# One of two x planes of a sampling step read back replicated from memory, the other double buffered in PSUM

## The chip, the cores and the metric

The kernel runs on one NeuronCore of a Trainium2 chip. The metric is the device time of one execution in microseconds (us). TensorE is called PE in the profile (its weight loads PEld), VectorE DVE, ScalarE ACT, GpSimd POOL and SyncE SP. SP issues the DMAs here.

## The reference

Four layers are added one after another onto x, of shape (4, 64, 48, 48), each on the group-normalised x: a deformable convolution (layer 1), two deformable convolutions that are mixed (layer 2), an attention (layer 3) and a convolution with generated weights (layer 4). The change is in layer 2, whose sampling is, cut to what matters:

```python
# offsets: B, 9 taps, (dy, dx), H, W, from a 3x3 convolution of x; twice, with two sets of weights
py = base_y + tap_y + dy;  px = base_x + tap_x + dx
sampled = bilinear_gather(x, py, px)          # B, C, 9, H, W; zero outside the image
out = einsum('bckhw,ock->bohw', sampled, w) + b
# the two results s0 and s1 are then mixed: wts0 * s0 + wts1 * s1 + conv1x1(x) * g
```

A bilinear gather is a sum over nearby pixels with the weight max(0, 1 - |y distance|) times max(0, 1 - |x distance|). The kernel uses this form where all offsets are small: every 4 x 6 tile of output pixels reads a window of 10 x 12 = 120 input pixels, and the gather is a matmul of the 120 window pixels with 120 x (pixels) weights.

## The kernel before

`windows1` works through 24 chunks of 8 rows of 48 pixels, so 384 pixels each (`CH`). There are 18 samples per pixel (9 taps of 2 convolutions), handled two at a time in 9 steps (`STEPS`).

**Hats.** For each chunk, PE computes the distances to the window's rows and columns for all samples ("place", line 1533, one matmul of 384 columns for each of 4 slots). ACT takes their magnitude (`magnitude`, 1617) into `temp`; POOL clips them (1705) and splits them into a high and a low f16 half (1708, 1710), the "hats". For the first chunk DVE does this (1662 to 1666). Hats are held compactly, 10 or 12 partitions for each sample, several samples to a slot and a group of 32 partitions.

**Spread** (1559). For step t PE replicates the y hats and the x hats of samples 2t and 2t+1 from 10 and 12 rows to the 120 window rows: four planes, each as a high and a low part, so eight matmuls of 32 rows x 120 columns in four row groups, four side by side. The y planes land in `p_y[t % 2]` (two banks each), the x planes in `p_x`, which has two banks and is single buffered.

**Weights.** A DVE operation can't take both factors from PSUM here, so ACT copies the first x plane to SBUF (`keep_x`, 1624), DVE copies the second (1672), and DVE then multiplies both y planes by both x planes in one operation of 768 columns (1677) into `bmat`.

**Sample** (1575). Eight times a chunk PE multiplies a pair of windows (loaded by SP at 1521 from `pixel_major` in DRAM) by the weights of the previous turn of `bmat`, into one of two banks `pq`, which the places use too; ACT moves the result to `smp` (`keep`, 1632).

**Conv** (1591) contracts 64 channels x 9 taps, 72 matmuls, into `pc` (in the banks of `p_y[1]`); ACT (1640) and DVE (1685) add the bias.

**Order.** All orders are written out by hand. PE runs, for chunk n: spread(n+1, t), sample(n, t), and after t in `PLACED = (0, 2, 4, 8)` a place for chunk n+2; then conv(n). ACT follows the same order with keep_x, keep and magnitude; DVE does the nine products of n+1 and then the bias of n; POOL has its own loop over the chunks and at the end normalises x again into `xn` for the next stage (1715). The spread waits for both copies of the step before:

```python
if g:
    pe.wait_ge(S["x0_out"], g)
    pe.wait_ge(S["x1_out"], g)
```

and conv(n) waits for the last keep, and for the products of n+1 up to the eighth. Of the places' turns and the samples' turns, each waits until the turn two before it has been emptied.

Of the kernel before, what the change touches and what calls it, by code (L numbers as in the profile page):

```python
# [4 lines left out]
F32 = mybir.dt.float32  # L5
U32 = mybir.dt.uint32
ALU = mybir.AluOpType
# [1439 lines left out]
def sample_slots():  # L1447


    groups = [(0, 1), (0, 2), (1, 2), (0, 3), (0, 1), (0, 2), (1, 3), (1, 2), (2, 3)]  # L1450
    places, rows = {}, {g: [] for g in range(4)}
    for axis, per, size in ((0, 3, IH + 6), (1, 2, IW + 6)):
        held = {g: [] for g in range(4)}
        for t, ys in enumerate(groups):
            own = ys if axis == 0 else [g for g in range(4) if g not in ys]
            for e, g in enumerate(own):
                held[g].append(2 * t + e)
# [6 lines left out]
    assert all(len(r) <= 4 for r in rows.values())  # L1464
# [3 lines left out]
def windows1(nc, k, o3, bmat, win, sc, smp, temp, xs):  # L1468
# [7 lines left out]
         ("loaded0", "loaded1", "hats0", "clipped0", "high0", "hats", "clipped", "high", "spread", "x0_out", "x1_out",  # L1476
          "weights", "filled", "emptied", "conv", "sc0", "sc1", "normed")}
# [4 lines left out]
    SLOTS = 4  # L1482
    places, _ = sample_slots()
    LAST = min(s // 2 for axis, s in places if places[axis, s][1] == SLOTS - 1)
# [9 lines left out]
    temp = temp.rearrange("p (q n) -> p q n", q=SLOTS)  # L1494

    PLACED = (0, 2, 4, STEPS - 1)

    def placing(n, t):

        return t in PLACED and n + 2 < NQ  # L1500

    turn_of = {("place", 0, q): q for q in range(SLOTS)}
    for n in range(-1, NQ):
        for t in range(STEPS):
            if n >= 0 and t < PAIRS:
                turn_of["sample", n, t] = len(turn_of)
            if placing(n, t):
                turn_of["place", n + 2, PLACED.index(t)] = len(turn_of)

    with nc.Block() as block:  # L1510
        @block.sync
        def _(sp):
            phased = k["xw"].rearrange("b y (j t) c -> b (y j) t c", j=IW)
            for n in range(NQ):
# [3 lines left out]
                for band in range(2):  # L1518
                    for a in range(2):
                        first = (ROWS * r + band * IH) * IW  # L1520
                        sp.dma_start(win[n % 2][KW // 2 * a:KW // 2 * (a + 1), band, :, :],
                                     phased[b, first:first + WH * IW, a:a + WW // IW, :]).then_inc(S[f"loaded{n % 2}"], 16)

        @block.tensor
        def _(pe):
# [10 lines left out]
            def spread(m, t):  # L1536
                g = m * STEPS + t
                held = SLOTS - 1 if t < LAST else SLOTS
                if m and t in (0, LAST):
                    pe.wait_ge(S["hats"], SLOTS * (m - 1) + held)  # L1540
                elif t in (0, LAST):
                    pe.wait_ge(S["hats0"], held)
                if g:
                    pe.wait_ge(S["x0_out"], g)
                    pe.wait_ge(S["x1_out"], g)
                if t < 2 and m:
                    pe.wait_ge(S["weights"], m * STEPS)
                elif t >= 2:
                    pe.wait_ge(S["weights"], g - 1)
                if t == 1 and m >= 2:  # L1550
                    pe.wait_ge(S["sc0"], m - 1)
                    pe.wait_ge(S["sc1"], m - 1)
                for part in range(2):
                    for axis in range(2):
                        for e in range(2):
                            row, slot, q = places[axis, 2 * t + e]
                            own = slice(32 * row, 32 * row + 32)
                            out = p_x[:, e, :] if axis else p_y[t % 2][:, e, :]
                            mm = pe.matmul(out, k["spr"][own, q, :], hat[m % 2][part][own, slot, :],  # L1559
# [1181 lines left out]
```

## Time and profile before

| what | value |
|---|---|
| runs (3), median | 1392.57 us |
| lowest, highest | 1387.49, 1393.74 us |
| profiled execution, span | 1386.4 us |
| PE busy | 1142.7 us |
| DVE busy | 983.5 us |
| ACT busy | 651.7 us |
| POOL busy | 696.3 us |
| first spread of the stage, end of its last instruction | 386.0 us, 788.5 us |

The profile gives the span of the profiled execution, from its first to its last recorded instruction, and no other time of it. The stage with the change takes 402 us of the 1386.4.

### The profile page before, as it was taken

Reading aid. Unit: us, or ns where it says so; the run is one execution under the profiler, and the core shown is the slowest. Engines: PE = TensorE matmul, PEld = TensorE weight load, DVE = VectorE, ACT = ScalarE, POOL = GpSimd, SP = SyncE. Lnnn points to the kernel's source line nnn. Section 1 sums busy time; section 2 is a strip of 40 time slices with the busy share of each in tenths; the row PEclk is TensorE's granted clock in tenths of the full one; section 3 lists DMA queues with packets and bytes.
Section 4 is the critical chain, followed back from the end, with each engine's and each line's share of the span. In section 5 each row is a group of like instructions: output and inputs, shape, how many; then the busy total and the mean of one; then the engine's idle time right before and its main releaser. Section 6 shows DMA issues by size and latency. Waiting matters only on the chain. (4 is left out here: it accounts for less than half of the span.)

```text
span 1386.4 us, 32503 instructions
## 1 busy us (share of the span) xinstructions
PE 1142.7 (82%) x13688; PEld 589.8 (43%) x13688; DVE 983.5 (71%) x1222; ACT 651.7 (47%) x1096; POOL 696.3 (50%) x549
## 2 busy tenths in 40 slices
PE   3970189869579999999999676699999999998658
PEld 2440177744225555555555443233333333334323
DVE  3788945567888888888888568746666666667623
ACT  1646035354546666666666535044444444445410
POOL 2000011203356767777676412078888888888600
PEclk9985599979769999999999889799999999999869
DMA  4100000001101111101111004000000000002002
GB/s 85 22 1 0 0 3 3 1 26 40 39 29 39 36 30 31 31 30 31 39 37 30 3 1 137 1 1 2 2 2 1 1 2 2 2 2 78 2 18 69
DMA packets 28884, 31.40 MB, mean 23 GB/s; under 512 B 19148, under 2 KB 21773, under 8 KB 27965
## 3 DMA queue, kind: packets, MB, share of 16 engines
q1 hardware_dynamic: 28573, 28.96, 7.9%
q8 instruction: 110, 1.80, 0.5%
q10 hardware_dynamic: 160, 0.30, 0.1%
q14 instruction: 41, 0.34, 0.1%
HBM read 20.91 MB, written 5.35 MB: 19 GB/s over the span
## 5 line engine op out<-in xcount | busy, mean ns | idle before, releaser
L2183 POOL TENSOR_TENSOR arena_sb<-arena_sb 128x768 f32<-128x768 f32 x168 | 322.5, 1920 | 119.6 <-ACT arena_sb L2144 99.1
L2144 ACT ACTIVATE arena_sb<-ps 128x768 f32<-128x768 f32 x216 | 175.0, 811 | 242.4 <-PE ps L2073 240.3
L2198 DVE TENSOR_REDUCE arena_sb<-ps 128x4 f32<-128x1536 f32 x108 | 188.2, 1756 | 128.8 <-PE ps L2040 128.3
L1677 DVE TENSOR_TENSOR arena_sb<-ps,arena_sb 120x768 f32<-120x768 f32 x216 | 206.8, 957 | 9.2
L2073 PE MATMUL ps<-arena_sb 33*64 33x384 f32 x1728 | 187.3, 502 | 11.4 <-ACT arena_sb L2144 5.5
L1705 POOL TENSOR_SCALAR xp_sb<-xp_sb 128x384 f32<-128x384 f32 x92 | 137.4, 1494 | 99.3 <-ACT xp_sb L1617 95.7
L1575 PE MATMUL ps<-arena_sb 120*64 120x216 f32 x1536 | 182.9, 360 | 0.0
L2085 PE MATMUL ps<-arena_sb 64*64 64x384 f32 x1728 | 168.0, 488 | 3.4 <-ACT arena_sb L2151 3.4
L1632 ACT ACTIVATE xp_sb<-ps 128x432 f32<-128x432 f32 x192 | 102.0, 531 | 63.1 <-PE ps L1575 63.1
L1559 PE MATMUL ps<-xn_sb,arena_sb 32*120 32x384 f16 x1728 | 120.8, 353 | 11.8 <-DVE arena_sb L1672 4.9
L1575 PEld LDWEIGHTS ps<-arena_sb 120*64 120x64 f32 x1536 | 93.4, 136 | 69.6 <-issue 32.9
L1672 DVE COPY arena_sb<-ps 120x384 f32<-120x384 f32 x216 | 118.8, 550 | 4.5 <-PE ps L1559 3.2
L2040 PE MATMUL ps<-arena_sb 32*128 32x384 f32 x864 | 104.6, 557 | 20.7 <-DVE arena_sb L2198 14.7
L1624 ACT ACTIVATE arena_sb<-ps 120x384 f32<-120x384 f32 x216 | 106.5, 493 | 17.6 <-PE ps L1559 14.0
L2073 PEld LDWEIGHTS ps<-arena_sb 33*64 33x64 f32 x1728 | 57.8, 134 | 110.4 <-ACT arena_sb L2144 86.2
L2085 PEld LDWEIGHTS ps<-arena_sb 64*64 64x64 f32 x1728 | 67.4, 134 | 78.8 <-issue 73.0
L1710 POOL TENSOR_TENSOR xn_sb<-xp_sb,xn_sb 128x384 f16<-128x384 f32 x92 | 84.5, 918 | 7.9
L1591 PE MATMUL ps<-xp_sb,arena_sb 64*64 64x192 f32 x1728 | 75.7, 325 | 6.1 <-DVE arena_sb L1677 5.5
L1559 PEld LDWEIGHTS ps<-xn_sb,arena_sb 32*120 32x120 f16 x1728 | 45.6, 129 | 76.3 <-ACT arena_sb L1624 45.9
L2040 PEld LDWEIGHTS ps<-arena_sb 32*128 32x128 f32 x864 | 35.6, 191 | 88.4 <-issue 44.9
L1591 PEld LDWEIGHTS ps<-xp_sb,arena_sb 64*64 64x64 f32 x1728 | 67.9, 133 | 11.7 <-ACT xp_sb L1632 11.5
L184 PE MATMUL ps<-x_sb,pairm_sb 128*128 128x256 f32 x56 | 22.2, 573 | 60.6 <-DVE arena_sb L573 60.6
(245 smaller groups left out, 1562.2 us busy)
## 6 DMA issues: line engine op xcount, KB each, us to landing
arena_sb<-pixel_major SPq DMA_DIRECT2D x96, 120.0 KB, 2.3
pixel_major<-arena_sb SPq DMA_DIRECT2D x24, 108.0 KB
x_sb<-in_x SPq DMA_DIRECT2D x4, 576.0 KB, 8.2
arena_sb<-arena_sb SPq DMA_DIRECT2D x8, 288.0 KB, 5.8
xn_sb<-in_W SPq DMA_DIRECT2D x1, 2304.0 KB, 8.0
arena_sb<-in_W SPq DMA_DIRECT2D x1, 2304.0 KB, 8.1
out_x<-x_sb SPq DMA_DIRECT2D x24, 96.0 KB, 2.2
arena_sb<-arena_sb SPq DMA_DIRECT2D x24, 1.5 KB
```

The source lines that it names most:

```text
L1559: mm = pe.matmul(out, k["spr"][own, q, :], hat[m % 2][part][own, slot, :], start=(part == 0), stop=(part == 1))
L1575: mm = pe.matmul(out[64 * v:64 * v + 64, :, :, IW * t:IW * t + IW], win[n % 2][0:KW, band, tile, :], weights[:, TAPS * v:TAPS * v + TAPS, ...
L1591: mm = pe.matmul(pc[v][64 * h:64 * h + 64, :], k["dws"][own, t, :], smp[own, at:at + CH // 2], start=(t == 0), stop=(t == TAPS - 1), skip_ ...
L1672: v_.tensor_copy(xs[t % 2][:, CH:2 * CH], p_x[:, 1, :]).then_inc(S["x1_out"], 1)
L1677: v_.tensor_tensor(bmat[m % 2][:, 2 * CH * t:2 * CH * t + 2 * CH].rearrange("p (e n) -> p e n", e=2), p_y[t % 2], xs[t % 2].rearrange("p ( ...
L1705: pool.tensor_scalar(temp[:, q, :], temp[:, q, :], UNIT, UNIT, ALU.min, ALU.subtract)\
L2040: mm = pe.matmul(p_m(m)[:, u, :], q4[own, CH * ib + PT * a:CH * ib + PT * a + PT], k4[own, CH * jc:CH * jc + CH], start=True, stop=True)
L2073: mm = pe.matmul(p_scores(g)[64 * i:64 * i + 64, h, :], kp[own, key:key + 64], qp[own, PIX * b2 + CH * ib:PIX * b2 + CH * ib + CH], start= ...
L2085: mm = pe.matmul(p_o[64 * h:64 * h + 64, i, :], at[64 * i:64 * i + 64, b2 * TPI + j, 64 * h:64 * h + 64], pt[g % SLOTS][64 * i:64 * i + 64 ...
L2144: act.activation(pt[g % SLOTS].rearrange("p (h n) -> p h n", h=2), p_scores(g), ACT.Exp)\
L2183: pool.tensor_tensor(acc, first, pt[g % SLOTS], ALU.add).then_inc(S["pool_added"], 1)
L2198: v.tensor_reduce(part.rearrange("p (a u j) -> p a u j", a=3, u=NB)[:, a, :, jc], p_m(m), AX.X, ALU.max)\
```

## The change

One of the two x planes of a step takes another way to the 120 window rows.

- The x hats of the nine odd samples ("far") get one slot of their own, 12 x 9 = 108 partitions of 384 values in f32. SP stores them in DRAM (`far_hats`) and reads them back in three blocks of three steps, each block in two DMAs of 60 partitions, with the source repeated ten times (`to_broadcast`), so that they arrive in SBUF on all 120 window rows (`xd[0..2]`). One block is reused when the chunk before is through with it.
- The compact hats then need three slots instead of four. There are still four places a chunk: far at the end of step 0, slots 0 and 1 at the end of steps 2 and 4, slot 2 inside step 6, ahead of its sample.
- A spread has six matmuls instead of eight. Its one x plane lands in `p_x[g % 2]`, two banks used in turn, so it no longer waits for copies of the step before.
- DVE drops its copy and its 768-wide product, and makes two products of 384: the odd sample's with `xd`, the even one's with ACT's copy, which has four buffers instead of two.
- The conv's output moves to the two banks `pq`, and the wait for the bias of the last conv moves from spread(1) to sample(0).
- POOL's normalisation into `xn` at the end waits for the last product as well, since `xd[0]` and `xd[1]` lie in `xn`.

```diff
@@ windows1
-    p_x = ps[0:KW, 2048:3072].rearrange("p (e n) -> p e n", e=2)[:, :, 0:CH]
+    p_x = [ps[0:KW, 512 * (4 + i):512 * (4 + i) + CH] for i in range(2)]
-    pc = [ps[:, 512 * (2 + v):512 * (2 + v) + CH // 2] for v in range(2)]
+    pc = [ps[:, 512 * (6 + v):512 * (6 + v) + CH // 2] for v in range(2)]
-    PLACED = (0, 2, 4, STEPS - 1)
+    def tail(n, i):
+        return n + 2 < NQ and i in HEADS[0:SLOTS]
+    def head(n, i):
+        return n + 2 < NQ and i == HEADS[SLOTS]
+    HEADS = (0, 2, 4, 6)
+    ORDER = (SLOTS,) + tuple(range(SLOTS))
@@ sync
+            def far_away(m):
+                if m:
+                    sp.wait_ge(S["far"], m)
+                else:
+                    sp.wait_ge(S["far0"], 1)
+                if m >= 2:
+                    for blk in range(3):
+                        sp.wait_ge(S[f"far_in{blk}"], 32 * (m - 1))
+                sp.dma_start(far_dram[m % 2], far).then_inc(S["far_out"], 16)
+
+            def far_back(m, blk):
+                if blk == 0:
+                    sp.wait_ge(S["far_out"], 16 * (m + 1))
+                if m:
+                    sp.wait_ge(S["weights"], (m - 1) * STEPS + BLOCK * (blk + 1))
+                lines = far_dram[m % 2].rearrange("(e t) n -> e (t n)", e=WX)
+                for a in range(2):
+                    src = lines[IW * a:IW * a + IW, BLOCK * CH * blk:BLOCK * CH * blk + BLOCK * CH]
+                    sp.dma_start(xd[blk][KW // 2 * a:KW // 2 * (a + 1), :],
+                                 src.unsqueeze(0).to_broadcast([WH, IW, BLOCK * CH])).then_inc(S[f"far_in{blk}"], 16)
+
+            window(0)
+            window(1)
+            far_away(0)
+            for blk in range(3):
+                far_back(0, blk)
+            for n in range(-1, NQ):
+                if n >= 1 and n + 1 < NQ:
+                    window(n + 1)
+                if n + 2 < NQ:
+                    far_away(n + 2)
+                    for blk in range(3):
+                        far_back(n + 2, blk)
@@ tensor, spread
-                if g:
-                    pe.wait_ge(S["x0_out"], g)
-                    pe.wait_ge(S["x1_out"], g)
-                if t < 2 and m:
-                    pe.wait_ge(S["weights"], m * STEPS)
-                elif t >= 2:
+                if g >= 2:
                     pe.wait_ge(S["weights"], g - 1)
-                if t == 1 and m >= 2:
-                    pe.wait_ge(S["sc0"], m - 1)
-                    pe.wait_ge(S["sc1"], m - 1)
                 for part in range(2):
-                    for axis in range(2):
-                        for e in range(2):
+                    for axis, e in ((0, 0), (0, 1), (1, 0)):
...
@@ tensor, sample and conv
                 if i == 0:
                     pe.wait_ge(S["weights"], (n + 1) * STEPS)
                     pe.wait_ge(S[f"loaded{n % 2}"], 64 * (n // 2 + 1))
+                    if n:
+                        pe.wait_ge(S["sc0"], n)
+                        pe.wait_ge(S["sc1"], n)
...
                 pe.wait_ge(S["emptied"], turn_of["sample", n, PAIRS - 1] + 1)
-                if n:
-                    pe.wait_ge(S["sc0"], n)
-                    pe.wait_ge(S["sc1"], n)
-                pe.wait_ge(S["weights"], (n + 1) * STEPS + (STEPS - 1 if n + 1 < NQ else 0))
@@ scalar
+                if q == SLOTS:
+                    if m:
+                        act.wait_ge(S["far_out"], 16 * m)
+                    act.activation(far, pq[u % 2][0:FAR, 0:CH], ACT.Abs).then_inc(S["emptied"], 1)
+                    return
...
-                if g >= 2:
-                    act.wait_ge(S["weights"], g - 1)
-                act.activation(xs[t % 2][:, 0:CH], p_x[:, 0, :], ACT.Copy).then_inc(S["x0_out"], 1)
+                if g >= XS:
+                    act.wait_ge(S["weights"], g - XS + 1)
+                act.activation(xs[g % XS], p_x[g % 2], ACT.Copy).then_inc(S["x0_out"], 1)
@@ vector, weight
-                v_.wait_ge(S["spread"], g + 1)
-                v_.tensor_copy(xs[t % 2][:, CH:2 * CH], p_x[:, 1, :]).then_inc(S["x1_out"], 1)
-                v_.wait_ge(S["x1_out"], g + 1)
-                v_.wait_ge(S["x0_out"], g + 1)
...
+                if at == 0:
+                    v_.wait_ge(S[f"far_in{blk}"], 32 * (m + 1))
+                v_.wait_ge(S["spread"], g + 1)
+                own = bmat[m % 2][:, 2 * CH * t:2 * CH * t + 2 * CH]
+                v_.tensor_tensor(own[:, CH:2 * CH], p_y[g % 2][:, 1, :], xd[blk][0:KW, CH * at:CH * at + CH], ALU.mult)
+                v_.wait_ge(S["x0_out"], g + 1)
+                v_.tensor_tensor(own[:, 0:CH], p_y[g % 2][:, 0, :], xs[g % XS], ALU.mult).then_inc(S["weights"], 1)
@@ gpsimd
+                pool.wait_ge(S["emptied"], turn_of["place", m, SLOTS] + 1)
+                pool.tensor_scalar(far, far, 1.0, 1.0, ALU.min, ALU.subtract).then_inc(S["far"], 1)
...
             pool.wait_ge(S["spread"], NQ * STEPS)
+            pool.wait_ge(S["weights"], NQ * STEPS)
```

`sample_slots` deals the samples anew over the groups of 32 rows, so that the three planes of a step always lie in three different groups.

## Rows read from the trace of the kernel before

**Rows 1.** The page: busy time of each engine over the span.

```profile
span 1386.4 us, 32503 instructions
PE 1142.7 (82%) x13688; PEld 589.8 (43%) x13688; DVE 983.5 (71%) x1222; ACT 651.7 (47%) x1096; POOL 696.3 (50%) x549
```

**Rows 2.** Busy time by window, two chunks from conv to conv.

```profile
core 0: us, PE busy (x) PEld busy (x) DVE busy (x) ACT busy (x) POOL busy (x), PEclk, DMA share, GB/s
546.54:562.70 16.16, 15.84 (x212) 8.93 (x212) 13.82 (x21) 10.63 (x25) 11.66 (x12) 1.00 0.11 32
562.70:578.87 16.17, 15.84 (x212) 8.94 (x213) 13.83 (x21) 10.63 (x25) 11.66 (x12) 1.00 0.11 32
```

**Rows 3.** Timeline, a chunk's end (start us, us, what, idle before it); one spread's first half.

```profile
556.32 0.95 PE L1575 MATMUL ps<-arena_sb 120*64 120x216 f32 x8
...
557.21 0.34 PE L1533 MATMUL ps<-arena_sb 109*128 109x384 bf16 x1
...
557.47 0.54 PE L1559 MATMUL ps<-xn_sb,arena_sb 32*120 32x384 f16 x8
...
557.94 0.95 PE L1575 MATMUL ps<-arena_sb 120*64 120x216 f32 x8
...
558.83 0.54 PE L1559 MATMUL ps<-xn_sb,arena_sb 32*120 32x384 f16 x8
...
559.59 0.55 DVE L1672 COPY arena_sb<-ps 120x384 f32<-120x384 f32 x1
...
560.21 0.22 PEld L1559 LDWEIGHTS ps<-xn_sb,arena_sb 32*120 32x120 f16 x8 [0.35 <-ACT arena_sb L1624]
...
560.71 0.95 PE L1575 MATMUL ps<-arena_sb 120*64 120x216 f32 x8
...
561.05 0.55 DVE L1672 COPY arena_sb<-ps 120x384 f32<-120x384 f32 x1
...
561.66 0.22 PEld L1559 LDWEIGHTS ps<-xn_sb,arena_sb 32*120 32x120 f16 x8 [0.39 <-ACT arena_sb L1624]
...
561.71 0.53 ACT L1632 ACTIVATE xp_sb<-ps 128x432 f32<-128x432 f32 x1 [0.39 <-PE ps L1575]
...
562.17 0.34 PE L1533 MATMUL ps<-arena_sb 109*128 109x384 bf16 x1
...
562.73 3.16 PE L1591 MATMUL ps<-xp_sb,arena_sb 64*64 64x192 f32 x72 [0.23 <-DVE arena_sb L1677]
...
565.82 0.54 PE L1559 MATMUL ps<-xn_sb,arena_sb 32*120 32x384 f16 x8
...
565.95 0.85 ACT L1640 ACTIVATE arena_sb<-ps,dbs_sb 64x192 f32<-64x192 f32 x2 [2.79 <-PE ps L1591]
...
566.29 0.95 PE L1575 MATMUL ps<-arena_sb 120*64 120x216 f32 x8
...
541.31 0.38 PE L1559 MATMUL ps<-xn_sb,arena_sb 32*120 32x384 f16 x4
```

**Rows 4.** Groups by line: an operation of DVE as wide as the new products.

```profile
L1342 DVE TENSOR_TENSOR arena_sb<-ps,arena_sb 108x384 f32<-108x384 f32 x24 | 11.7, 550 | 5.6 <-PE ps L1269 5.2
```

**Rows 5.** Timeline, the end of the stage.

```profile
772.27 16.28 POOL L1715 TENSOR_SCALAR xn_sb<-x_sb,stats_sb 128x2304 f32<-128x2304 f32 x2 [12.04 <-PE ps L1559]
...
776.73 0.53 ACT L1632 ACTIVATE xp_sb<-ps 128x432 f32<-128x432 f32 x1
777.31 0.56 PEld L1575 LDWEIGHTS ps<-arena_sb 120*64 120x64 f32 x8 [0.29 <-ACT xp_sb L1632]
...
786.01 0.85 DVE L1685 TENSOR_SCALAR arena_sb<-ps,dbs_sb 64x192 f32<-64x192 f32 x2 [9.30 <-PE ps L1591]
```

**Rows 6.** DMAs: issues, windows while window loads run, packets of the first eight.

```profile
381.30 3.50 SPq L1521 DMA_DIRECT2D arena_sb<-pixel_major  x8
...
arena_sb<-pixel_major SPq DMA_DIRECT2D x96, 120.0 KB, 2.3
arena_sb<-arena_sb SPq DMA_DIRECT2D x8, 288.0 KB, 5.8
...
547.00:549.00 2.00, 2.00 (x56) 2.00 (x52) 0.88 (x1) 0.00 (x0) 1.85 (x2) 1.00 0.62 193
381.00:385.00 4.00, 1.70 (x4) 0.34 (x4) 2.73 (x7) 1.74 (x4) 0.00 (x0) 0.50 0.57 170
...
DMA packets 600, 0.98 MB, mean 164 GB/s; under 512 B 120, under 2 KB 120, under 8 KB 600
```

**Rows 7.** Timeline, the stage's first and ninth product and its first sample.

```profile
387.72 0.96 DVE L1677 TENSOR_TENSOR arena_sb<-ps,arena_sb 120x768 f32<-120x768 f32 x1
...
400.77 0.96 DVE L1677 TENSOR_TENSOR arena_sb<-ps,arena_sb 120x768 f32<-120x768 f32 x1
...
401.85 0.31 PEld L1559 LDWEIGHTS ps<-xn_sb,arena_sb 32*120 32x120 f16 x8 [1.68 <-issue]
402.71 1.01 PEld L1575 LDWEIGHTS ps<-arena_sb 120*64 120x64 f32 x8 [0.55 <-issue]
```

More of the change, by code:

```diff
@@ L1447, in sample_slots @@
 def sample_slots():
-    groups = [(0, 1), (0, 2), (1, 2), (0, 3), (0, 1), (0, 2), (1, 3), (1, 2), (2, 3)]
+    steps = [(0, 1, 2), (0, 1, 3), (0, 2, 1), (1, 2, 0), (0, 3, 1), (1, 3, 0), (0, 1, 2), (0, 3, 2), (1, 2, 3)]
     places, rows = {}, {g: [] for g in range(4)}
-    for axis, per, size in ((0, 3, IH + 6), (1, 2, IW + 6)):
+    for axis, per in ((0, 3), (1, 2)):
         held = {g: [] for g in range(4)}
[L1454 to L1457, printed above, removed]
+        for t, (first, second, across) in enumerate(steps):
+            for g, s in ((first, 2 * t), (second, 2 * t + 1)) if axis == 0 else ((across, 2 * t),):
+                held[g].append(s)
         for g in range(4):
@@ L1463, in sample_slots, with windows1 @@
                     places[axis, s] = (g, slot, q + 3 * axis)
-    assert all(len(r) <= 4 for r in rows.values())
+    assert all(len(r) <= SPREAD_SLOTS for r in rows.values())
     return places, rows
-def windows1(nc, k, o3, bmat, win, sc, smp, temp, xs):
+SPREAD_SLOTS = 3
+FAR = WX * TAPS
+def windows1(nc, k, o3, bmat, win, sc, smp, temp, xs, xd):
     ps = k["psum"]
     S = {n: signal(k, "win_" + n) for n in
-         ("loaded0", "loaded1", "hats0", "clipped0", "high0", "hats", "clipped", "high", "spread", "x0_out", "x1_out",
-          "weights", "filled", "emptied", "conv", "sc0", "sc1", "normed")}
+         ("loaded0", "loaded1", "hats0", "clipped0", "high0", "far0", "hats", "clipped", "high", "far", "far_out",
+          "far_in0", "far_in1", "far_in2", "spread", "x0_out", "weights", "filled", "emptied", "conv", "sc0", "sc1",
+          "normed")}
     NQ = NB * CPI
@@ L1513, in _, with window @@
             phased = k["xw"].rearrange("b y (j t) c -> b (y j) t c", j=IW)
-            for n in range(NQ):
+            def window(n):
                 b, r = divmod(n, CPI)
@@ L1659, in _ @@
         def _(v_):
+            v_.wait_ge(S["emptied"], turn_of["place", 0, SLOTS] + 1)
+            v_.tensor_scalar(far, far, 1.0, 1.0, ALU.min, ALU.subtract).then_inc(S["far0"], 1)
             for q in range(SLOTS):
@@ L2709 @@
                     selp[R3, slot, at] = -e
+    for e in range(WX):
+        for t in range(TAPS):
+            selp[0:R3, SPREAD_SLOTS, TAPS * e + t] = row == 2 * (2 * t + 1) + 1
+            selp[R3, SPREAD_SLOTS, TAPS * e + t] = -e
     for q in range(3):
```

100 lines of the change are left out of this document (58 added, 42 removed).

## The prediction

> **What bounds the kernel now.** The page first [rows 1]: TensorE (PE) is busy 82% of a 1386.4 us span, VectorE (DVE) 71%. The change touches only layer 2's sampling, so I went from the page to the busy time by window over two of its 24 chunks [rows 2]: one chunk takes 16.16 us, and in it PE is busy 15.84, DVE 13.82, ACT 10.63, POOL 11.66, at full granted clock. PE's 0.3 us of idle is not all of its slack, since the pace of matmuls that wait for weights doesn't show as idle. So the third view is the timeline of the end of one chunk [rows 3], read for the distance from the start of one PE group to the start of the next:
>
> - sample to place 0.89 (556.32 to 557.21), place to spread 0.26, spread to sample 0.47, sample to spread 0.89 (557.94 to 558.83) where nothing holds it.
> - In the two steps without a place the last distance is 0.95 and 0.99. There the weight load of the spread starts at 560.21 and 561.66, right behind the end of the copy of the second x plane (559.59 + 0.55 = 560.14; 561.05 + 0.55 = 561.60). This is the single x buffer: the spread may not overwrite `p_x` before both copies are out. DVE meanwhile runs copy and product end on end, one step per 1.46 us.
> - At the chunk's end place to conv takes 0.56 instead of 0.26, until DVE's product at line 1677 lets go.
> - The conv to the next spread takes 3.09, and sample(0) follows 0.47 later, before the two bias operations (565.95 to 566.80) are done.
>
> The unheld sum of a chunk is conv 3.09 + 9 spreads x 0.47 + 8 samples x 0.88 + 4 places x 0.265 = 15.42 (the finer end of 0.88 to 0.89 and 0.26 to 0.27 is taken; with 0.89 it is 15.5). Against 16.16 the waits on DVE's copies and products are worth 0.7 us a chunk, 17 us over 24 chunks. That is all the change can win in the steady part by relieving DVE.
>
> **Steps that are taken off DVE and PE.** DVE loses the copy (0.55) and its 768-wide product (0.96) and gets two products of 384 columns; the nearest row with one PSUM and one SBUF operand and 384 columns is 0.55 [rows 4], so 1.10 or less instead of 1.51, 3.7 us a chunk. That is no gain by itself: PE is then alone on the path. A spread goes from eight matmuls to six, but they are four (now three) side by side in two rounds: the first four of one spread take 0.38 us together and a single place with the same 384 columns 0.34 [rows 3], so a matmul more or less in a round costs (0.38 - 0.34)/3 = 0.013. Its bounds: 0, and 2 x 0.013 x 216 = 5.7 us won over the kernel. I take 0, since the distance from spread to sample (0.47) is the same as from spread to place and looks set by two rounds and a drain, not by the count.
>
> The Trainium skill ("TensorE: Matmul & The Clock Gate", Part 3, Measured speedup vs the span model) says that row tiles side by side cost one matmul plus about 4 ns for each further tile. By that rule the removed pair is worth 8 ns a spread, an estimate of 1.7 us in all, and the trace's 0.38 against 0.34 is of that order.
>
> **Waits that are added.** The conv's output moves from `p_y`'s banks to the two banks `pq` in which samples and places land. Two things follow.
>
> - sample(0) of the next chunk now waits for both biases of the conv. They start 3.22 after the conv (565.95 against 562.73) and last 0.85, so they end at +4.07; a weight load starts 0.05 after such a release (776.73 + 0.53 = 777.26, load at 777.31 [rows 5]). sample(0) starts at +4.12 instead of +3.56: 0.56 us of PE with nothing behind it to fill, because spread(1) is queued behind sample(0).
> - The conv still waits for ACT's keep of sample(7), which ends 1.53 after that sample's start (560.71 to 561.71 + 0.53 = 562.24). Up to now a spread (0.89 + 0.47) and a place (0.26) filled 1.62. The place of step 8 moves to the head of step 6, so only 1.36 is filled, and with 0.06 to 0.08 of release the conv starts 1.60 after the sample: 0.24 lost.
>
> New chunk: 15.42 + 0.56 + 0.24 = 16.22, with the coarse sum 16.30; I take 16.26, 0.10 more than now. Over the 22 chunks that have both a conv behind and spreads ahead: +2.2 us. Bounds of this term: 16.16 - 0.2 if the rounds get cheaper, which is -4, and 16.16 + 0.3 (+7) if the coarser distances hold and ACT, which has a magnitude and a keep_x ahead of keep(6), holds sample(6) up by a tenth.
>
> **Work at no cost, and its cover.** POOL has three slots (1.49 + 0.50 + 0.92 each) and one 1.49 for the far planes, 10.2 us instead of 11.66; the last slot, placed at step 6, is done about 1.4 us before the next chunk begins, and is needed at its step 2 only. ACT has the same number of operations. SP gets one store and six reads more per chunk (about 0.5 us of issue each, by 8 issues in 3.50 us [rows 6]); window(n+1) stands behind them but has a whole chunk of cover. The read-back moves 6 x 276 KB a chunk. Its first pair can start once the far store has landed, about 10 us after the conv, and is needed at about 20 us; the later pairs have 11. A 120 KB load lands in 2.3 us, a 288 KB transfer of another layer in 5.8 [rows 6]: hidden either way. If the cover were gone, each microsecond beyond it would cost 22.
>
> **The ends of the stage.** Before the first product the far planes must go out and come back. SP issues eight window loads first (381.30 to about 385.2), then the store (landing 2.3, at 387.5), then the first pair. With 553 KB at the 193 GB/s of a window stretch (2.9 us), and 1.7 for a landing's fixed part (2.3 less 0.6 for its 120 KB) [rows 6], they land about 4.7 us later, at 392.2, where now the first product starts at 387.72 and the ninth ends at 401.73 [rows 7]. Nine steps at 1.05 end at 401.7, and spread(1,0) need no longer wait for all nine (now it starts at 401.85), so sample(0) goes from 402.71 to 401.7: -1 us. Bounds: -3.4 (the pair lands in 2.3) to +2.5 (the store takes 5.8). At the other end POOL's normalisation, 16.28 us from 772.27 to 788.55, ends the stage, 1.7 us after ACT and DVE (786.01 + 0.85) [rows 5]. It waits now for the last spread and will wait for the last product too: two products of 0.55 more, +1.1. The 0.6 us that the last chunk's sample(0) waits and the conv's 0.24 lie under it.
>
> Sum: +2.2 - 1.0 + 1.1 = +2.3 us on a span of 1386.4. The profile gives no other time of that execution; the median of the runs is 1392.57, 6.2 above the span, and I carry that over: 1394.9, say 1395.
>
> **The rivals.**
>
> - *The wait was worth more than its replacement* (faster). If spreads of three tiles are quicker by the share of instructions removed, 2/8 of 0.47 = 0.12 a spread, 216 of them save 25 us: 1370. At the upper bound from the rows above (5.7) it is 1389. For it: PE is what paces the new chunk. Against it: the 0.38 beside 0.34. Chance 0.18, most of it between 1375 and 1386.
> - *The read-back paces the chunk* (slower). 480 KB of windows, 166 KB out and 1656 KB back are 2.3 MB in 16.26 us, 141 GB/s. The stretches of window loads show 193 GB/s at a DMA share of 0.62, and 170 in one that starts idle [rows 6]. It decides below 141 GB/s; at 120 a chunk takes 19.2 us and the kernel 1395 + 22 x 2.9 = 1459. For it: reads whose source repeats ten times are in no row of this kernel. Against it: both stretches of window loads are above the limit though SP issues only one 120 KB load per half microsecond in them, and a read-back carries 276 KB per issue. Chance 0.10, with a few small stalls of DVE (each under 1 us a chunk, to 1415) in it.
> - *ACT comes late* (slower): in the steps with a place sample(i+1) starts 0.05 behind the release of keep(i), so anything ahead of a keep costs its full length. A tenth at four places a chunk is 0.4 x 23 = 9 us: 1404. Chance 0.12.
> - *The change trades nothing visible*: the forecast, 0.60, with its own range 1388 to 1400.
>
> The page that speaks against the change is "DMA: Bandwidth & Descriptors" of the Trainium skill (Rules for kernel authors): a leading zero-stride broadcast of c copies confines a DMA to at most c engines, here ten. The trace agrees as far as it goes: the eight window loads, 60 rows each, carry 120 packets under 512 B, 15 each, the largest divisor of 60 up to 16. By that rule the read-back runs at ten sixteenths of 193/0.62 = 311 GB/s, an estimate of 195 GB/s: 8.5 us a chunk for the 1656 KB, which would not change the sum; did it bind, the time would be the second rival's.
>
> **How the numbers follow.** The likeliest case gives 1395. The range 1383 to 1405 takes in the bounds of the terms (-4 to +7 for the chunks, -3 to +3 for the start, -5.7 for the rounds) and the ACT case, and leaves out most of the first and second rival. About 0.5%, 7 us, is what a measurement of this kernel can tell from no change: faster than 1385.6 has 0.18, slower than 1399.5 has 0.24 (0.10 + 0.12 + the forecast's own tail), the rest 0.58.
>
> **What would show it.** In the changed profile: conv to conv 16.2 to 16.3; copies gone and DVE about 10 us busy a chunk; the weight load of sample(0) held for 0.5 to 0.6 us by the biases of ACT and DVE, that of the conv by ACT's keep; spread to sample still 0.47; DMA share 0.3 to 0.5 with no DVE wait on a DMA after the first chunk; POOL's normalisation starting 1.7 us after the last spread. The prediction is wrong if spread to sample falls below 0.45, if DVE waits for a DMA in each chunk, or if sample(0) isn't held.

## The result and the profile after

The changed kernel takes 1401.56 us (median of 7 runs, 1397.21 to 1401.63), the kernel before 1391.75 in the same comparison (7 runs, 1387.14 to 1394.44). The ratio is 1.0067, 95% interval 1.0048 to 1.0086: slower by 0.67%, 6.7 to 12 us. The prediction was 1395 within 1383 to 1405. The time lies inside, 6.6 above the centre, and falls under "slower by over 0.5%", which had been given 0.24 against 0.58 for no visible change.

The page of the changed kernel answers to [rows 1]; the profiled execution took 1401.58, 1.8 above its span:

```profile
span 1399.8 us, 31420 instructions
PE 1143.0 (82%) x13256; PEld 589.2 (42%) x13256; DVE 901.1 (64%) x1220; ACT 646.2 (46%) x1096; POOL 664.5 (47%) x503
```

DVE lost 82 us of work and the profiled span is longer. Busy time by window over two chunks from conv to conv, against [rows 2]:

```profile
core 0: us, PE busy (x) PEld busy (x) DVE busy (x) ACT busy (x) POOL busy (x), PEclk, DMA share, GB/s
541.50:557.92 16.42, 15.55 (x195) 8.66 (x195) 10.56 (x21) 10.38 (x24) 10.23 (x11) 1.00 0.51 149
557.92:574.34 16.42, 15.55 (x194) 8.66 (x194) 10.56 (x21) 10.38 (x24) 10.23 (x11) 1.00 0.48 140
```

A chunk takes 16.42 us where 16.26 was predicted and 16.16 was the time before; DVE went from 13.82 to 10.56, 3.3 less, where 3.7 and "about 10" were said. PE is busy 0.29 less and idle 0.87 instead of 0.32. The timeline shows where, from one conv (L1635) over the first samples (L1623) to the next conv:

```profile
541.50 3.15 PE L1635 MATMUL ps<-xp_sb,arena_sb 64*64 64x192 f32 x72 [0.16 <-ACT xp_sb L1684]
...
544.58 0.54 PE L1604 MATMUL ps<-xn_sb,arena_sb 32*120 32x384 f16 x6
544.72 0.85 ACT L1692 ACTIVATE arena_sb<-ps,dbs_sb 64x192 f32<-64x192 f32 x2 [2.85 <-PE ps L1635]
544.72 0.85 DVE L1743 TENSOR_SCALAR arena_sb<-ps,dbs_sb 64x192 f32<-64x192 f32 x2 [2.26 <-PE ps L1635]
...
545.79 0.59 PEld L1623 LDWEIGHTS ps<-arena_sb 120*64 120x64 f32 x8 [1.03 <-issue]
545.82 0.95 PE L1623 MATMUL ps<-arena_sb 120*64 120x216 f32 x8 [0.71 <-DVE arena_sb L1743]
...
547.44 0.95 PE L1623 MATMUL ps<-arena_sb 120*64 120x216 f32 x8
...
548.79 0.95 PE L1623 MATMUL ps<-arena_sb 120*64 120x216 f32 x8
...
556.34 0.95 PE L1623 MATMUL ps<-arena_sb 120*64 120x216 f32 x8
...
557.22 0.54 PE L1604 MATMUL ps<-xn_sb,arena_sb 32*120 32x384 f16 x6
557.34 0.53 ACT L1684 ACTIVATE xp_sb<-ps 128x432 f32<-128x432 f32 x1 [0.39 <-PE ps L1623]
...
557.92 3.15 PE L1635 MATMUL ps<-xp_sb,arena_sb 64*64 64x192 f32 x72 [0.16 <-ACT xp_sb L1684]
```

Read it as three pieces. From conv to sample(0) 4.32 (541.50 to 545.82). From sample(0) to sample(7) 10.52, made of steps of 1.62 with a place and 1.35 without (545.82, 547.44, 548.79): that is 0.88 + 0.47, with 0.27 for a place, so nothing holds these steps any more. From sample(7) to the conv 1.58, released by ACT's keep (557.34 + 0.53 = 557.87). The first piece was priced at 4.12, and here the price is missed: the biases end at 545.57, 4.07 after the conv as forecast, but the weight load comes at 545.79, 0.22 behind them, not 0.05, and the first matmul 0.03 behind the load. (4.12 was the start of the load, while the 3.56 of before that it was set against is the start of the matmul; in the kernel before the two start together.)

The start of the stage in the timeline, against [rows 6] and [rows 7]:

```profile
385.42 0.81 PE L1587 MATMUL ps<-arena_sb 109*128 109x384 bf16 x2 [1.35 <-PEq L1372]
385.69 3.49 SPq L1541 DMA_DIRECT2D arena_sb<-pixel_major  x8
...
389.22 0.36 SPq L1552 DMA_DIRECT2D far_hats<-xp_sb  x1
...
391.99 3.28 SPq L1562 DMA_DIRECT2D xn_sb<-far_hats  x4
...
397.41 0.56 DVE L1735 TENSOR_TENSOR arena_sb<-ps,xn_sb 120x384 f32<-120x384 f32 x1 [6.69 <-DMA xn_sb<-far_hats]
...
406.78 0.28 PEld L1604 LDWEIGHTS ps<-xn_sb,arena_sb 32*120 32x120 f16 x6 [1.55 <-POOL xn_sb L1770]
...
407.61 1.01 PEld L1623 LDWEIGHTS ps<-arena_sb 120*64 120x64 f32 x8 [0.55 <-DVE arena_sb L1737]
...
409.00 0.56 DVE L1735 TENSOR_TENSOR arena_sb<-ps,xn_sb 120x384 f32<-120x384 f32 x1 [1.92 <-DMA xn_sb<-far_hats]
```

DVE waits 6.69 us for the first pair of read-backs. The code ahead of the stage is unchanged but its end scatters (the first place lay at 381.0 to 386.7 us in the profiles of this study), so all positions below count from the first place of the stage: sample(0) comes at 22.19, and came at 21.67 before. DVE's ninth product ends at 407.08, but sample(0) is queued behind spread(1,0), which waits until 406.78 for POOL's hats and takes 0.83 at the lower clock. So sample(0) starts at 407.61, 0.53 behind DVE's end; with 0.05 to 0.22 for a release, 0.3 to 0.5 of that is POOL's doing. Its end, against [rows 5]:

```profile
787.94 16.27 POOL L1776 TENSOR_SCALAR xn_sb<-x_sb,stats_sb 128x2304 f32<-128x2304 f32 x2 [14.19 <-DVE arena_sb L1737]
```

POOL's normalisation starts 1.63 us after the last spread (the start of its second round; 0.44 before), and from there to the end of the stage it takes 17.90 instead of 16.72.

### The profile page after: what moved, and what is told of

The parts are those of the page before. It is cut to its first block and busy times, and to the rows that moved or that the text cites. A ratio compares the mean times of both kernels' runs of the same rounds, so it can differ in the third digit from the quotient of the medians.

```text
span 1399.8 us, 31420 instructions
## 1 busy us (share of the span) xinstructions
PE 1143.0 (82%) x13256; PEld 589.2 (42%) x13256; DVE 901.1 (64%) x1220; ACT 646.2 (46%) x1096; POOL 664.5 (47%) x503
## 5 line engine op out<-in xcount | busy, mean ns | idle before, releaser
L1623 PE MATMUL ps<-arena_sb 120*64 120x216 f32 x1536 | 185.8, 364 | 16.8 <-DVE arena_sb L1743 16.8
L1623 PEld LDWEIGHTS ps<-arena_sb 120*64 120x64 f32 x1536 | 96.6, 138 | 85.4 <-issue 44.2
L1765 POOL TENSOR_SCALAR xp_sb<-xp_sb 128x384 f32<-128x384 f32 x69 | 103.0, 1493 | 48.9 <-ACT xp_sb L1669 45.1
L1735 DVE TENSOR_TENSOR arena_sb<-ps,xn_sb 120x384 f32<-120x384 f32 x144 | 80.3, 558 | 70.0 <-PE ps L1604 60.7
L1737 DVE TENSOR_TENSOR arena_sb<-ps,arena_sb 120x384 f32<-120x384 f32 x216 | 120.2, 556 | 1.1
L1758 POOL TENSOR_SCALAR xp_sb<-xp_sb 108x384 f32<-108x384 f32 x23 | 34.4, 1494 | 96.0 <-ACT xp_sb L1663 96.0
L1635 PE MATMUL ps<-xp_sb,arena_sb 64*64 64x192 f32 x1728 | 75.7, 325 | 4.4 <-ACT xp_sb L1684 4.4
L1604 PEld LDWEIGHTS ps<-xn_sb,arena_sb 32*120 32x120 f16 x1296 | 41.6, 131 | 71.0 <-issue 63.1
L1635 PEld LDWEIGHTS ps<-xp_sb,arena_sb 64*64 64x64 f32 x1728 | 63.7, 133 | 16.5 <-ACT xp_sb L1684 12.8
```

What stands on the lines that cost most here:

```text
L1623: mm = pe.matmul(out[64 * v:64 * v + 64, :, :, IW * t:IW * t + IW], win[n % 2][0:KW, band, tile, :], weights[:, TAPS * v:TAPS * v + TAPS, ...
L1635: mm = pe.matmul(pc[v][64 * h:64 * h + 64, :], k["dws"][own, t, :], smp[own, at:at + CH // 2], start=(t == 0), stop=(t == TAPS - 1), skip_ ...
L1737: v_.tensor_tensor(own[:, 0:CH], p_y[g % 2][:, 0, :], xs[g % XS], ALU.mult).then_inc(S["weights"], 1)
L1765: pool.tensor_scalar(temp[:, q, :], temp[:, q, :], UNIT, UNIT, ALU.min, ALU.subtract)\
```

## The experiments

Theory A: the two waits that the conv brought with it into `pq` eat the gain, and sample(0)'s release costs 0.17 more than it was priced at. Theory B: the read-back's traffic slows what lies beside it (0.50 of the DMA engines busy at 142 GB/s, where it was 0.11 and 32 [rows 2]). A third, A2, was for the first profile's chunk 0: TensorE came to its full granted clock 15.0 us after sample(0), against 4.4 before, and the theory is that its idle time while DVE waits for the read-back delayed the clock. e1 to e4 and e7 to e9 are edits to the changed kernel; e5 builds on e1, and e6 on e5. In all of them `p_x` and `p_y` stay twice buffered. Where an edit has one run, its effect is read from the distances in its trace and not from its time.

**e1_conv_home: the conv back in two banks of `p_y`.** With it the waits go back: spread(1) waits for the biases, spread(0) and the conv for the products that empty the banks.

```diff
-    pc = [ps[:, 512 * (6 + v):512 * (6 + v) + CH // 2] for v in range(2)]
+    pc = [ps[:, 512 * (2 + v):512 * (2 + v) + CH // 2] for v in range(2)]
...
+                if t < 2 and m:
+                    pe.wait_ge(S["weights"], m * STEPS)
+                if t == 1 and m >= 2:
+                    pe.wait_ge(S["sc0"], m - 1)
+                    pe.wait_ge(S["sc1"], m - 1)
...
-                        out = p_x[g % 2] if axis else p_y[g % 2][:, e, :]
+                        out = p_x[g % 2] if axis else p_y[t % 2][:, e, :]
...
-                    if n:
-                        pe.wait_ge(S["sc0"], n)
-                        pe.wait_ge(S["sc1"], n)
```

> The changed kernel with the conv's output put back into the banks of the second y buffer and the wait for the bias back in spread(1), so sample(0) no longer waits for it; the y buffers go by the step's number again. The rest of the change stays. Theory A (the two banks of the conv cost the chunk its gain): in the changed kernel's trace sample(0) starts 4.32 us after the conv, here 3.55, so a chunk takes 15.65 us instead of 16.42, 17 us less over 22 chunks: about 1385, 7 us below the kernel before. Theory B (the read-back, 1.66 MB a chunk, paces the stage): the wait moves to another place, a chunk stays at 16.4 and the time at 1401. If the conv's own wait for the products of step 7 bites, a chunk takes up to 15.9 and the kernel 1390.

Measured: 1384.4 us median (1379.19 to 1386.74) beside 1390.16 of before, ratio 0.9955 (0.9939 to 0.997). A chunk takes 15.65 us:

```profile
549.24 3.16 PE L1641 MATMUL ps<-xp_sb,arena_sb 64*64 64x192 f32 x72 [0.16 <-ACT xp_sb L1690]
...
552.33 0.54 PE L1609 MATMUL ps<-xn_sb,arena_sb 32*120 32x384 f16 x6
552.47 0.85 ACT L1698 ACTIVATE arena_sb<-ps,dbs_sb 64x192 f32<-64x192 f32 x2 [2.85 <-PE ps L1641]
...
552.79 0.38 PEld L1625 LDWEIGHTS ps<-arena_sb 120*64 120x64 f32 x6 [0.28 <-issue]
```

sample(0) starts at 552.79, while the biases of 552.47 still run: 3.55 after the conv, 0.77 earlier than the 4.32 of the changed kernel, and 0.77 is what the chunk became shorter by (16.42 to 15.65). The same read-backs and products now win. So the relief of DVE is worth what the prediction said (16.16 - 15.65 = 0.51 with 0.23 of the conv's wait still there), and the wait of sample(0) alone, 0.77, was larger than it.

**e2_bias_wait_last: the bias waits behind the wait for the sample's bank.**

```diff
-                    if n:
-                        pe.wait_ge(S["sc0"], n)
-                        pe.wait_ge(S["sc1"], n)
                 u = turn_of["sample", n, i]
                 empty(u)
+                if i == 0 and n:
+                    pe.wait_ge(S["sc0"], n)
+                    pe.wait_ge(S["sc1"], n)
```

> The changed kernel; only the order of sample(0)'s waits differs: the wait for the bias comes behind those for the weights, the window and the bank. In the changed kernel sample(0)'s weight load starts 0.22 us after the bias has ended, with two wait instructions 0.11 apart between them. If each wait instruction behind the late one costs, the load comes 0.11 to 0.17 earlier and a chunk takes 16.26 to 16.31 instead of 16.42: 2 to 4 us in all. If the 0.22 is a fixed price of this release, conv to conv stays at 16.42.

One run of 1398.54; a chunk takes 16.42 as before the edit:

```profile
555.52 0.85 ACT L1692 ACTIVATE arena_sb<-ps,dbs_sb 64x192 f32<-64x192 f32 x2 [2.85 <-PE ps L1635]
555.52 0.85 DVE L1743 TENSOR_SCALAR arena_sb<-ps,dbs_sb 64x192 f32<-64x192 f32 x2 [2.26 <-PE ps L1635]
...
556.59 0.23 PEld L1623 LDWEIGHTS ps<-arena_sb 120*64 120x64 f32 x4 [1.02 <-issue]
```

The biases end at 556.37, the weight load comes at 556.59, 0.22 later. The wait instructions of TensorE's queue in the trace tell why: the five waits of sample(0) stand as two in each of two wait instructions and one in the load itself. In the changed kernel both biases are in the first wait instruction; with this edit one of them is still there, and only the other is in the second. So the edit didn't do what it was meant to, and it says nothing on the price of a wait instruction; e9 does.

**e3_thin_read_back: only 128 of 1152 columns read back** for all chunks but the first (x planes incomplete, so the weights are other numbers).

```diff
+                    W_ = 128 if m else BLOCK * CH
...
-                                 src.unsqueeze(0).to_broadcast([WH, IW, BLOCK * CH]))
+                                 src.unsqueeze(0).to_broadcast([WH, IW, W_]))
```

> The changed kernel with the same DMAs and waits, but from the second chunk on each read-back brings 128 of the 1152 columns of its block (512 B instead of 4608 B a row), so most x weights of the odd samples are stale. Theory B: a chunk falls from 16.42 towards 15.5 us, 15 us or more in all. Theory A: the transfers are hidden, conv to conv stays at 16.42 within 0.02, and only the DVE wait of 1.9 us in the second chunk goes.

One run of 1400.99. Busy time by window over the steady part, the changed kernel first, then this one:

```profile
405.00:770.00 365.00, 345.72 (x4193) 189.85 (x4192) 231.23 (x439) 227.64 (x504) 226.22 (x223) 0.98 0.50 142
```

```profile
405.00:770.00 365.00, 345.59 (x4264) 191.11 (x4262) 234.89 (x446) 229.54 (x509) 230.68 (x227) 0.99 0.17 52
```

DMA falls from 0.50 to 0.17 of the engines and from 142 to 52 GB/s; conv to conv stays at 16.43, and of the DVE waits on a DMA only the 1.92 us one in chunk 0 goes. Theory B falls: these bytes are free here (the number of DMAs was left as it is).

**e4_clock_kept: twenty matmuls more in DVE's wait for the first read-back**, into a bank that a place overwrites.

```diff
+                    if n == -1 and i == 1:
+                        pe.wait_ge(S["emptied"], SLOTS + 1)
+                        for _ in range(20):
+                            pe.matmul(pq[1][:, 0:CH], k["selp"][:, 0, :], o3[:, 0:CH], start=True, stop=True)
```

> The changed kernel with 20 matmuls of 384 columns of no use put behind spread(0,1), in the 6.9 us in which TensorE waits for the first read-back. In the changed kernel the granted clock rises to full only 14.4 us after the first sample, in the kernel before 4.3 us after it, and from the first sample to the first conv it takes 18.8 us instead of 14.4. Theory A2 (the idle stretch for the read-back keeps the clock down): full clock by the first sample, first sample to first conv about 13 to 14.5 us, 4 to 6 us less in all. Rival (the clock rises late because a spread holds fewer matmuls, or by chance of its phase): first sample to first conv stays near 18.8.

One run of 1400.87. Windows of the stage's start (the column behind POOL's is the granted clock):

```profile
394.00:398.00 4.00, 3.58 (x16) 1.69 (x14) 0.00 (x0) 0.11 (x1) 1.33 (x1) 0.76 0.51 141
398.00:402.00 4.00, 1.40 (x16) 0.56 (x19) 3.00 (x7) 1.25 (x3) 0.29 (x1) 1.00 0.67 218
402.00:406.00 4.00, 3.85 (x29) 1.27 (x32) 3.76 (x8) 2.36 (x6) 3.77 (x4) 0.59 0.29 98
406.00:410.00 4.00, 2.81 (x20) 1.21 (x20) 2.01 (x4) 1.47 (x3) 3.70 (x5) 0.50 0.61 185
410.00:414.00 4.00, 4.00 (x29) 1.64 (x27) 2.33 (x5) 2.10 (x5) 2.46 (x3) 0.63 0.65 181
```

The extra matmuls bring the full clock 9.6 us after the first place, but it is gone again at 402.7 (16.4 after the first place) and comes back at 26.7, 4.2 after sample(0). e3, without such matmuls, has it 3.7 after its sample(0). So the late clock of the first profile is no necessary effect of the change, and A2 doesn't explain it; the repetitions below settle that.

**e5_home_place_last: e1, and the place back behind step 8**, where the conv's wait was filled.

```diff
-        return n + 2 < NQ and i in HEADS[0:SLOTS]
+        return n + 2 < NQ and i in HEADS
...
-    HEADS = (0, 2, 4, 6)
+    HEADS = (0, 2, 4, STEPS - 1)
```

> The kernel of the first experiment (conv in the y buffer's banks) with the fourth place back behind step 8, ahead of the conv, instead of inside step 6. There the conv of the first experiment must wait for ACT's keep of sample(7), 1.6 us behind that sample's start, while a spread fills only 1.36. If that wait is real and the place fills it, a chunk takes 15.42 us, the unheld sum of the prediction, instead of 15.65, and the kernel 5 us less: 1379. If the conv is held by the products instead, it stays at 15.65 and 1384.

1377.03 us median (1376.21 to 1379.12) beside 1391.33, ratio 0.9902 (0.9885 to 0.9918). The chunk's end:

```profile
545.54 0.95 PE L1625 MATMUL ps<-arena_sb 120*64 120x216 f32 x8
...
546.42 0.54 PE L1609 MATMUL ps<-xn_sb,arena_sb 32*120 32x384 f16 x6
...
546.89 0.34 PE L1587 MATMUL ps<-arena_sb 109*128 109x384 bf16 x1
...
547.16 3.16 PE L1641 MATMUL ps<-xp_sb,arena_sb 64*64 64x192 f32 x72
```

Spread and place now fill the whole way from sample(7) to the conv, which shows no idle time ahead of it. Conv to conv is 15.42, the unheld sum that the prediction had put together from single distances.

**e6_all_mended: e5, with e7's and e8's edits.** 

> The kernel above with two more edits: the first far store and its read-backs are issued ahead of the first eight window loads, and the first half of POOL's normalisation no longer waits for the last product (its half of the array holds no read-back block). Expected against the kernel above: 2 to 3 us off the start (the store goes out at about 1.5 us behind the first place instead of 3.8) and 1.2 us off the end: 1375 to 1377, about 1.1% below the kernel before. If the start is set by the clock and not by the read-back, only the 1.2 us at the end show.

1374.57 us median (1373.91 to 1379.31), ratio 0.9885 (0.9868 to 0.9901): the fastest version. The chunk is e5's 15.42, the stage 394.37 us long against 396.86 in e5. In both profiles the full clock comes at nearly the same place (36.0 and 36.2 us from the first place), so they can be compared from the start on: conv(0) is 1.3 earlier in e6, and the end gives the other 1.2.

**e7_norm_split: the first half of POOL's normalisation no longer waits for the last product.** In the edit the wait for `weights` moves into the loop, ahead of the second half only.

```diff
-            pool.wait_ge(S["weights"], NQ * STEPS)
             st = k["stats"]
             for b in range(2):
+                if b:
+                    pool.wait_ge(S["weights"], NQ * STEPS)
```

> The changed kernel with only the second half of POOL's normalisation waiting for the last product. In the changed kernel it starts 1.65 us behind the start of the last spread's last round and ends 18.1 us behind the last spread's start; before it was 16.9. Expected: 16.9 again, 1.2 us off the stage. If the end of the stage is set by TensorE's last conv instead, nothing is won.

One run of 1394.91. From the last spread to the end of the stage it takes 16.72 again, and POOL's row names the spread as its releaser:

```profile
781.31 16.27 POOL L1777 TENSOR_SCALAR xn_sb<-x_sb,stats_sb 128x2304 f32<-128x2304 f32 x2 [13.02 <-PE ps L1604]
```

**e8_far_first: the first far store and its read-backs ahead of the window loads.**

```diff
-            window(0)
-            window(1)
             far_away(0)
             for blk in range(3):
                 far_back(0, blk)
+            window(0)
+            window(1)
```

> The changed kernel with the first far store and its read-backs issued ahead of the first eight window loads. In the changed kernel the store goes out 3.8 us behind the first place, DVE's first product starts 12.0 us behind it, and the first sample 22.2. Theory: the first product comes 2.3 us earlier, at 9.7, and the first sample at about 20. Rival: POOL's hats of the second chunk hold spread(1,0) (it waited 1.55 us for them in the changed kernel), then the first sample comes less than 1 us earlier.

One run of 1400.21. The timeline:

```profile
388.06 3.28 SPq L1562 DMA_DIRECT2D xn_sb<-far_hats  x4
391.38 1.52 SPq L1562 DMA_DIRECT2D arena_sb<-far_hats  x2
392.95 4.07 SPq L1541 DMA_DIRECT2D arena_sb<-pixel_major  x8
394.08 0.56 DVE L1735 TENSOR_TENSOR arena_sb<-ps,xn_sb 120x384 f32<-120x384 f32 x1 [4.35 <-DMA xn_sb<-far_hats]
397.06 0.36 SPq L1552 DMA_DIRECT2D far_hats<-xp_sb  x1
403.85 3.15 SPq L1562 DMA_DIRECT2D xn_sb<-far_hats  x4
...
409.23 0.56 DVE L1735 TENSOR_TENSOR arena_sb<-ps,xn_sb 120x384 f32<-120x384 f32 x1 [5.49 <-DMA xn_sb<-far_hats]
```

The first product comes 9.64 us after the first place (384.44) instead of 11.99, and sample(0) at 19.84, 2.4 earlier. But the next chunk's store now goes out behind the eight window loads, 12.6 after the first place instead of 11.5. Its read-back follows 6.8 later, as it did in the changed kernel (6.6; only the stage's first store took 2.8), so DVE waits 5.49 us in chunk 0 and starts that product at 24.8 instead of 23.6. Whether anything is won by conv(0) this profile can't tell against e11 and e12: it is at 38.8 with the full clock 33.2 after the first place, they at 36.4 with the clock at 26.7 and 26.9. Beside the first profile of the changed kernel, whose clock was late too (37.1), conv(0) is 2.2 earlier. e6 against e5, with equal clocks, puts the gain of this edit at 1.3 in that version.

**e9_early_waits: two of the five waits ahead of sample(0) moved up in TensorE's queue**, ahead of the spread before it, where both have long been met.

```diff
                 if i == 0:
-                    pe.wait_ge(S["weights"], (n + 1) * STEPS)
-                    pe.wait_ge(S[f"loaded{n % 2}"], 64 * (n // 2 + 1))
+                    if n == 0:
+                        pe.wait_ge(S["weights"], (n + 1) * STEPS)
+                        pe.wait_ge(S[f"loaded{n % 2}"], 64 * (n // 2 + 1))
...
+                    if n > 0 and i == 0:
+                        pe.wait_ge(S["weights"], (n + 1) * STEPS)
+                        pe.wait_ge(S[f"loaded{n % 2}"], 64 * (n // 2 + 1))
```

> The changed kernel with sample(0)'s waits for the weights and the window moved ahead of spread(0) of the same turn, where both are met already (except in the first chunk). Behind the conv sample(0) then has three waits instead of five. In the run with the bias wait last nothing changed, and its trace showed why: the waits are packed two to a wait instruction, one of the two bias semaphores still in the first of them, and a second wait instruction 0.11 us behind it. If the number of wait instructions behind the late semaphore is the price, the load starts 0.11 us earlier and conv to conv falls from 16.42 to 16.31, 2.4 us in all. If not, it stays at 16.42.

One run of 1392.16; a chunk takes 16.27. Around sample(0):

```profile
549.62 3.15 PE L1636 MATMUL ps<-xp_sb,arena_sb 64*64 64x192 f32 x72 [0.16 <-ACT xp_sb L1688]
...
552.85 0.85 DVE L1747 TENSOR_SCALAR arena_sb<-ps,dbs_sb 64x192 f32<-64x192 f32 x2 [2.26 <-PE ps L1636]
...
553.77 0.56 PEld L1624 LDWEIGHTS ps<-arena_sb 120*64 120x64 f32 x7 [0.87 <-ACT arena_sb L1696]
```

The biases end at 553.70 and the load follows at 553.77, 0.07 behind them instead of 0.22. The chunk is 0.155 shorter, and all of it is here. One wait instruction stands between the late biases and the load where there were two, and it was reached early: the trace shows it from 551.88 to 553.74, with one of the biases in it and the other in the load.

**e10_before_again, e11_after_again, e12_home_last_norm: repetitions**, the kernel before once and the changed kernel twice (e12 too is the changed kernel without an edit, whatever its label says).

> The kernel before, once more with a profile, for the scatter of what the change doesn't touch. In its first profile the first place came 381.0 us after the start and the clock rose 4.4 us behind the first sample, with the first conv 36.1 us behind the first place. If the late clock is a matter of the execution and not of the change, some of these looks differ from the first by several us; conv to conv stays at 16.16.

> The changed kernel once more. In its first profile the clock rose 15.0 us behind the first sample and the first conv came 41.0 us behind the first place; in the second, fourth and seventh experiment, whose start is the same up to there, 36.5 to 37.9. Expected if it is a matter of the execution: 36.5 to 38 here; if it belongs to this kernel: 41. Conv to conv stays at 16.42.

> A second repetition of the changed kernel, for the same purpose: a third look at where the clock rises behind the first sample (15.0 us in the first) and at the place of the first conv (41.0 us); the same two outcomes.

Single runs of 1393.97 (before), 1397.83 and 1396.41 (changed); another run of before beside them took 1389.51. One window of chunk 0, in the first profile of the changed kernel and then in e11:

```profile
411.00:415.00 4.00, 4.00 (x23) 1.55 (x19) 1.79 (x4) 1.41 (x4) 0.86 (x1) 0.50 0.50 161
```

```profile
411.00:415.00 4.00, 4.00 (x42) 1.75 (x38) 2.82 (x6) 2.90 (x8) 2.31 (x3) 1.00 0.15 46
```

Granted clock 0.50 (the lower level, 1.2 GHz) in the one, 1.00 in the other, in the same program. The stage, in us from its first place:

| profile | sample(0) | full clock after sample(0) | conv(0) | conv to conv | last spread | end |
|---|---|---|---|---|---|---|
| before | 21.67 | 4.4 | 36.09 | 16.16 | 390.79 | 407.51 |
| e10 (before again) | 21.66 | 4.7 | 36.19 | 16.16 | 390.83 | 407.55 |
| changed | 22.19 | 15.0 | 41.01 | 16.43 | 400.89 | 418.79 |
| e11 (changed again) | 22.35 | 4.5 | 36.49 | 16.43 | 396.36 | 414.26 |
| e12 (changed again) | 22.28 | 4.4 | 36.37 | 16.43 | 396.15 | 414.05 |
| e8 | 19.84 | 13.4 | 38.81 | 16.43 | 398.60 | 416.49 |
| e5 | 23.74 | 12.2 | 41.12 | 15.42 | 378.97 | 396.86 |
| e6 | 19.77 | 16.4 | 39.82 | 15.42 | 377.66 | 394.37 |

With equal clocks the change costs 414.15 - 407.53 = 6.6 us in its stage. No run rules out that the change makes a late clock more frequent: both profiles of the kernel before have it early, and four of the twelve others (the first one, e5, e6 and e8) have it 12 us or more after sample(0), e1 11.8.

## Why the prediction was right or wrong

**Right: the mechanism, and the size of the relief.** The relief of DVE removes the holds inside the steps (every step from sample(0) to sample(7) is unheld), and two new waits give it back. The unheld sum of 15.42 was measured as such in e5; the conv's wait for the keep, 1.60 predicted, is 1.58; sample(0) is held by the biases.

**Wrong: the size of sample(0)'s release.** The term was "+4.12", with 0.05 from the end of the biases to the weight load, read off a load that waits for one ACT operation [rows 5]. Measured: 4.32, with 0.22 and the 0.03 from the load to its matmul. Five waits stand ahead of sample(0), both late ones in the first of two wait instructions; with two of the five moved ahead the distance is 0.07 (e9). The chunk came to 16.425, the 16.22 of its fine sum and these 0.20, instead of the 16.26 that was taken: 0.26 over the 16.16 before instead of 0.10. Over the 22 chunks this term is 5.8 instead of 2.2; in the profiles 21 distances of 0.26 make 5.5, and the distance from conv(21) to conv(22), in which no place stands, gave 0.6 back.

**Wrong: the start, by 1.6.** The step was "-1.0", by a first product 11.2 us after the first place. It comes at 11.99: the store took 2.8 to its read-back (389.22 to 391.99; 2.3 taken), the pair 5.4 (391.99 to 397.41) where 4.7 was taken. Nine steps of 1.07 follow, where 1.05 was said. And spread(1,0), said to be free of the products, waits 1.55 for POOL's hats (L1770), a wait that the sum left out and that costs sample(0) 0.3 to 0.5. sample(0) is at 22.2 to 22.4 in the three profiles of the changed kernel, +0.6 and inside the bounds of -3.4 to +2.5. Half of it doesn't reach conv(0), which is +0.3 in e11 and e12.

**Right: the rest.** Six matmuls cost what eight cost: spread to sample is 0.47 in both kernels. The Trainium skill ("TensorE: Matmul & The Clock Gate", Part 3, Measured speedup vs the span model) has about 4 ns for each further tile, 8 ns for the removed pair; the medians here are 471 ns with four tiles a round and 468 with three, so the trace has even less. The read-back is hidden (e3), with no DVE wait on a DMA after the first chunks. Where nothing but read-backs moves, over 553 to 557, it goes at 173 GB/s and a DMA share of 0.59, below the 195 of the prediction's estimate and still enough. The stretch holds 20 packets under 512 B, 10 for each of two landings, where a window load has 15, which fits the prediction's ten engines. The tail is +1.2 (17.90 - 16.72), +1.1 predicted, and e7 takes it back. All four steps with a place take 1.62, the unheld 0.88 + 0.27 + 0.47, so the rival of ACT fell too, as did that of cheaper spreads.

**The account.** Predicted in the stage: +2.2 - 1.0 + 1.1 = +2.3. Measured with equal clocks: +0.3 to conv(0), +4.8 from there to conv(22), +1.5 behind that (the tail's 1.2 in it), 6.6. The medians are 9.8 apart. The remaining 3.2 is not settled. The first profile had 4.6 us more ahead of conv(0) with the late clock, and its time, 1401.58, is one of four at 1401.6 while the other three are at 1397.2 to 1399.4; that these four all had the late clock was not shown, and a time like theirs doesn't need it: e3 and e4, with the clock at 3.7 and 4.2 and stages of 414.1 us, took 1400.99 and 1400.87. In the profiles the code ahead of the stage differs by up to 5.7 us and what follows it by up to 5.1 (595.5 to 600.6), more than the 3.2 to be explained. Single runs of the kernel before also lie 4.5 apart (1389.51 and 1393.97). Of the 6.6 between centre and result, 4.3 are mis-sized terms; the rest is the unsettled 3.2, less the 0.8 by which the kernel before was faster in this comparison. The chances failed by how near the centre stood to the bound: with the 6.6 of the stage it would have been 1392.57 + 6.6 = 1399.2, at the edge of 1399.5. The time lies inside the range with or without the unsettled part. The range was 22 us wide for the sake of rivals that didn't come, so that it held says little of the sum.

## What to carry to other kernels

When an engine is relieved, look at where the freed buffer came from: here the second x bank cost the conv its own banks, and one hold of 0.77 us a chunk and 0.23 of the conv's wait that a moved place no longer filled cost more than the 0.74 us of relief. The same relief with the conv left in banks that are empty anyway gave 0.45%, 1.0% with the place left in the conv's wait, and 1.15% with start and end mended. Price a release not only by the end of the work waited for but also by the wait instructions between the late wait and the instruction, and move the waits that have long been met to an earlier instruction. A work item that fills a wait is worth its length only where it stands.

## What the runs showed of the hardware

- Waits of TensorE's queue have a price. From the end of the last bias to the weight load: 0.05 us with one wait [rows 5], 0.07 in e9 with three waits, 0.22 with five, in the changed kernel and in e2. Order as such stays untested, since in e2 one of the two late waits is still in the first wait instruction.
- Reads whose source repeats ten times ran at 142 GB/s (with the rest of the traffic) over 365 us at a DMA share of 0.50 and cost the compute engines nothing that conv to conv shows. Their latency counts only at the stage's start: DVE's first product came 5.4 us after the first pair of 270 KB each was issued. The store of 162 KB ahead of them took 2.8 us to its read-back the first time, and 6.6 the second time, when it was issued right behind the first six read-backs.
- The full granted clock came 3.7 to 16.4 us after the first sample across the profiles, and 15.0 and 4.5 us in two executions of one program. From sample(0) to conv(0) it took 18.8 us in the one and 14.1 in the other, so a single profile can't be read for its first chunk.
